# Products that nobody reads, in TensorE's waits between the end of attention and the sort of a one-core decoder layer

## What is computed

```python
x = x + linear_attention(layernorm(x))            # 16 heads, running sums of k v over the 64 rows
x = x + autocorrelation_attention(layernorm(x), ctx)   # see below
x = x + moe_ffn(layernorm(x))                     # 8 experts, top 2, sort by expert, gated up and down products
```

## Time and profile before

| | |
|---|---|
| median of three runs | 636.89 us (636.69 to 638.78) |
| the profiled execution's own time | 637.31 us |
| its span, first to last instruction | 635.5 us |
| TensorE busy | 570.0 us, 90% of the span |
| VectorE (DVE) busy | 517.7 us, 81% |
| GpSimd (POOL) busy | 427.1 us, 67% |
| ScalarE (ACT) busy | 420.1 us, 66% |
| mean granted TensorE clock | 0.947 of full speed |
| TensorE's share of the chain that ended last | 62% |

### The profile page before, as it was taken

One profiled execution on the slowest core, in us unless ns is written; L12 is line 12 of the kernel. 1 busy time (PEld: TensorE's weight loads), 2 busy tenths in 40 slices (PEclk: granted clock), 3 DMA queues, 4 the chain that ended last, 5 costly groups with the idle time before them and its releaser, 6 DMA issues.

```text
span 635.5 us, 15657 instructions
## 1 busy us (share of the span) xinstructions
PE 570.0 (90%) x3750; PEld 448.5 (71%) x3751; DVE 517.7 (81%) x1602; ACT 420.1 (66%) x1188; POOL 427.1 (67%) x461
## 2 busy tenths in 40 slices
PE   3899999999999999786899767799999999999993
PEld 1455555555555555455789754599999999989993
DVE  5699999999999999972678878566778887877883
ACT  4557877877787775441788512344788888878882
POOL 3899989998999899110877600765367666756762
PEclk9999999999999999955799859999999999999998
DMA  5510111111161111363477542222012111111110
GB/s 147 190 43 0 35 33 36 33 33 33 33 99 33 34 33 35 86 98 87 118 206 203 111 102 38 49 49 50 23 50 53 47 47 51 49 40 47 55 44 23
DMA packets 49972, 40.90 MB, mean 64 GB/s; under 512 B 21971, under 2 KB 40278, under 8 KB 49926
## 3 DMA queue, kind: packets, MB, share of 16 engines
q1 hardware_dynamic: 44150, 29.61, 18.8%
q0 software_dynamic: 4960, 10.49, 6.3%
q10 hardware_dynamic: 816, 0.26, 0.2%
HBM read 27.47 MB, written 12.88 MB: 63 GB/s over the span
## 4 chain that ended last, share of the span: by engine, by line
PE 62%; ACT 13%; DVE 12%; issue 6%; DMA 3%; POOL 2%; DVEq 0%; ACTq 0%; POOLq 0%; SPq 0%
PE bank L1329 55%; PE bank L1333 4%; ACT xh L671 3%; ACT xs L773 2%; DVE on L935 2%; PE bank L1545 2%; ACT nb_c L668 1%; ACT ex L647 1%; PE bank L1468 1%; DMA shared<-xs_d,row_u 1%; DVE R L896 1%; ACT rl L648 1%; ACT xrT L759 1%; ACT ex L653 1%; ACT v L650 1%
## 5 line engine op out<-in xcount | busy, mean ns | idle before, releaser
L542 POOL TENSOR_TENSOR shared<-v,qk 128x1152 f32<-128x1152 f32 x64 | 142.7, 2230 | 2.8
L1329 PE MATMUL bank<-shared,tri_s 128*128 128x360 f32 (+1 forms) x384 | 136.3, 491 | 0.8 <-DVE R L896 0.8
L609 POOL DMA_INDIRECT shared<-xs_d,row_u x91 | 87.9, 966 | 64.0 <-DVE row_u L1227 32.7
L896 DVE TENSOR_TENSOR R<-bank,qk 128x360 f32<-128x360 f32 (+1 forms) x192 | 96.1, 540 | 7.4 <-PE bank L1329 5.5
L1329 PEld LDWEIGHTS bank<-shared,tri_s 128*128 128x128 f32 x384 | 69.5, 192 | 44.9 <-issue 20.4
L616 POOL DMA_INDIRECT out_x<-shared x64 | 63.5, 993 | 48.3 <-DVE shared L1299 21.7
L905 DVE TENSOR_REDUCE nd<-R 128x144 f32<-128x1152 f32 x64 | 86.2, 1347 | 1.6
L1329 PE MATMUL bank<-w_s,hid 128*128 (+1 forms) x620 | 82.3, 276 | 0.0
L1329 PEld LDWEIGHTS bank<-w_s,hid 128*128 128x128 f32 x620 | 75.5, 192 | 0.6 <-issue 0.3
L812 ACT ACTIVATE shared<-bank 128x256 f32<-128x256 f32 x155 | 59.4, 384 | 21.7 <-PE bank L1329 16.2
L1320 DVE TENSOR_TENSOR hid<-bank,shared 128x256 f32<-128x256 f32 x155 | 61.6, 422 | 11.6 <-ACT shared L812 11.6
(11 more groups left out here) (245 smaller groups left out, 1146.0 us busy)
## 6 DMA issues: line engine op xcount, KB each, us to landing
xs_d<-xs SPq DMA_DIRECT2D x16, 270.0 KB, 5.0
X<-in_x SPq DMA_DIRECT2D x16, 256.0 KB, 2.8
ct<-in_ctx_t SPq DMA_DIRECT2D x16, 256.0 KB, 2.9
ct<-in_ctx_r SPq DMA_DIRECT2D x16, 256.0 KB, 3.6
gram_d<-gd SPq DMA_DIRECT2D x14, 256.0 KB, 2.4
w_s<-in_w_experts SPq DMA_DIRECT2D x8, 384.0 KB, 3.9
circ<-prob_d SPq DMA_DIRECT2D x30, 64.0 KB, 2.7
shared<-xs_d,row_u POOLq DMA_INDIRECT x91, 2.5
```

What stands on the lines that cost most here:

```text
L542: nc.gpsimd.tensor_tensor(outer[k], v9[k % 2][:].unsqueeze(3).broadcast_to([P, H, D1, D]), kk.unsqueeze(2).broadcast_to([P, H, D1, D]), AL ...
L609: nc.gpsimd.indirect_dma_start(xg[q], None, xs_d[:, :], bass.IndirectOffsetOnAxis(ap=rows, axis=0)).then_inc(xg_in[q], 16)
L896: nc.vector.tensor_tensor(R[:, lo:hi], bank[2 + c][:, 0:n_h * D1 * D].rearrange("p (h e d) -> p h e d", h=n_h, e=D1), qq.unsqueeze(2).broa ...
L1329: return nc.tensor.matmul(o, l, r, start=start, stop=stop, skip_group_check=True)
```

## The change

`keep_warm` moves ahead of the slots and takes a bank and a number. Its operands become `ones3` on both sides (bf16 ones, 128 x 128, the moving side read four times over, so 512 columns as before). It is called at twelve more places, which makes 88 more products in all: 10, 2, 6 and 2 in slots 16 and 17 of attention (bank 2, which the running sums have left; a wait on `b_mul` stands ahead of the first); 18 between the mean's early and late product, 6 ahead of the fifth value product and 8 behind it (bank 7); 3 behind each of the circulant products 0 to 3 (bank 7); 4 behind the last circulant product, 5 at the start of slots 16 and 17, 3 behind the counts of slot 16, 3 and 4 behind those of slot 18 (bank 0). The calls in the sort keep bank 5 and their numbers.

```diff
--- before.py
+++ after.py
@@ -1348,6 +1348,11 @@
                 need(pe, a_pev, 3 * t)
                 mm(bank[1][:, 0:3 * E], xT[:, k * P:(k + 1) * P], wqkv[:]).then_inc(a_proj, 1)
 
+            def keep_warm(of, times):
+
+                for _ in range(times):
+                    mm(bank[of][:], ones3[:], ones3[:].unsqueeze(1).broadcast_to([P, 512 // P, P]))
+
             def slot(n, i):
                 a1, b, c, d = (stage(n, i, s) for s in (1, 0, -1, -2))
                 if i is None and n == 0:
@@ -1379,9 +1384,14 @@
                     mm(bank[7][:], wkk[:, 0:E], ct[p][:]).then_inc(d_k, 1)
                 if a1:
                     project(*a1, 1)
+                if i is None and n == NG:
+                    pe.wait_ge(b_mul, 3 * NT)
+                    keep_warm(2, 10)
                 if c:
                     pe.wait_ge(c_on, c[0] + 1)
                     transposes(bank[5], on).then_inc(c_tr, 1)
+                if i is None and n == NG:
+                    keep_warm(2, 2)
                 if b:
                     running_sums(*b, 2)
                 if c:
@@ -1398,8 +1408,12 @@
                     project(*a1, 2)
                 if d:
                     g, p, r = d
+                    if i is None and g == NG - 1:
+                        keep_warm(2, 6)
                     pe.wait_ge(d_xh, GT * g + GT)
                     transposes(bank[5], xh2).then_inc(d_tr, 1)
+                    if i is None and g == NG - 1:
+                        keep_warm(2, 2)
                 if b:
                     running_sums(*b, 3)
                 if a1:
@@ -1442,14 +1456,20 @@
                 v_product(*grp(g))
             pe.wait_ge(mean_ch, 1)
             mm(bank[4][:, 0:L], ones_f[:], mean_early[:], True, False)
+            keep_warm(7, 18)
             pe.wait_ge(mean_ch, MEAN_READY)
             mm(bank[4][:, 0:L], ones_f[:], mean_late[:], False, True).then_inc(mean_mm, 1)
             mm(bank[3][:, 0:L], late_of, mean_late[:]).then_inc(mean_mm, 1)
             for g in range(EARLY_V, PRE):
+                if g == PRE - 1:
+                    keep_warm(7, 6)
                 v_product(*grp(g))
+            keep_warm(7, 8)
 
             def cross_slot(n):
                 v, e, f, sc = (cross_stage(n, k) for k in (1, 0, -2, -3))
+                if n in (NG, NG + 1):
+                    keep_warm(0, 5)
                 if e:
                     g, p, r = e
                     pe.wait_ge(e_u, g + 1)
@@ -1458,6 +1478,10 @@
                     for k in range(GT):
                         last = mm(bank[2][:, k * P:(k + 1) * P], circ[p][:, k, :], u_of(g)[:, k, :])
                     last.then_inc(e_y, 1)
+                    if g < PRE - 1:
+                        keep_warm(7, 3)
+                    if g == NG - 1:
+                        keep_warm(0, 4)
                 if v and v[0] >= PRE:
                     v_product(*v)
                 if f:
@@ -1485,20 +1509,19 @@
                         last = mm(counts[:, (k + 1) * NPAIR:(m + 1) * NPAIR], ones_b[:],
                                   picked[:, t + k:t + k + 1, 0:NPAIR].broadcast_to([P, m - k, NPAIR]), False, k == m - 1)
                     last.then_inc(s_cnt, 1)
+                    if t + m == NT:
+                        keep_warm(0, 4)
+                    elif n >= NG:
+                        keep_warm(0, 3)
 
             pe.wait_ge(setup, 11)
             cross_slots(cross_slot)
-
-            def keep_warm(times):
-
-                for _ in range(times):
-                    mm(bank[5][:], ones_b[:], picked[:, 0:512 // NPW, :])
 
             pe.wait_ge(r_ch, START_READY)
             mm(bank[0][:, 0:NPAIR], ones_f[0:NPAIR, :], wide_f[0:NPAIR, 0:NPAIR]).then_inc(r_mm, 1)
             pe.wait_ge(r_ch, TILE_READY)
             mm(bank[2][:, 0:NXI], ones_f[0:NPAIR, :], wide_f[0:NPAIR, NPAIR:2 * NPAIR]).then_inc(r_mm, 1)
-            keep_warm(16)
+            keep_warm(5, 16)
             for b in range(NT // NSORT):
                 pe.wait_ge(o_low, b + 1)
                 pe.wait_ge(o_part, b + 1)
@@ -1507,15 +1530,15 @@
                     last = mm(bank[1][:, 0:P], is_row[b % 2][:, k // 2, :, :, k % 2], is_low[b % 2][:, k // 2, :, k % 2],
                               b + k == 0, b * NSORT + k == NT - 1)
                 last.then_inc(o_mm, 1)
-                keep_warm(4 if b < NT // NSORT - 1 else 2)
+                keep_warm(5, 4 if b < NT // NSORT - 1 else 2)
             pe.wait_ge(r_ch, ROWS_READY)
             mm(bank[3][:, 0:NT + NXI], row_t, select[:]).then_inc(r_mm, 1)
             pe.wait_ge(r_ch, BEGUN_READY)
             mm(bank[4][:, 0:5 * NT], ones_f[0:NPAIR, :], begun[0:NPAIR].rearrange("p m j -> p (m j)")).then_inc(r_mm, 1)
-            keep_warm(4)
+            keep_warm(5, 4)
             pe.wait_ge(r_ch, MASK_READY)
             nc.tensor.transpose(bank[6][:, 0:P], new_mask[:], id_s[:]).then_inc(r_mm, 1)
-            keep_warm(6)
+            keep_warm(5, 6)
 
             packs_pe = [None, None]
 
```

## The result

| | before | after |
|---|---|---|
| runs, median | 638.23 us (6 runs, 636.69 to 638.78) | 633.38 us (6 runs, 632.29 to 634.77) |
| profiled execution | 637.31 us, span 635.5 | 633.54 us, span 631.7 |

The ratio is 0.9928 with an interval of 0.9912 to 0.9944: faster by 0.7%, against the 633.1 us forecast. The changed kernel was run again beside the experiments (e0): 633.08 us, ratio 0.9904 [0.9875, 0.9934].

What follows compares the result with a forecast made beforehand. PE at half clock was taken to bound nearly every PE step from 267 to 309 us, besides DMA, and the last groups from 360 to 372. Gains 0.81 + 0.31 + 1.11 + 2.0 = 4.23 off 637.31 gave 633.1, range 631.4 to 636.8.

Steps and rivals of the forecast that it cites:

- Transposes, products, last gram: End of attention: everything behind the output products 1.5 us earlier, 2.4 us with the last gram; its dummies cost nothing.
- The open wait: Between the value products and the early mean's product: PE has nothing for 2.9 us, without a dummy.
- The 18 dummies: Between early and late mean's product: they block the late one for 1.6 us, so it gains 0.81 instead of 2.4.
- Late product to DVE's next step: From the late mean's product to DVE's next step: 0.73 us becomes 0.42, a gain of 0.31.
- Store and load of the weights: DVE and two DMAs up to the first circulant product: 8.74 us unchanged, PE's work hidden with about 0.9 us margin.
- Circulant products: Circulant products 0 to 3: the first saves 0.91 us, the next transposes just 0.2, together 1.11.
- Last slots: Last transposes and scores ahead of DVE's last choice: DVE starts 2.05 us earlier, taken as 2.0.
- the fall in the open wait: Rival, 0.24: clock falls ahead of the early mean's product, 6 to 13 dummies run slow; 634.2 to 635.9 us.
- All given back: Rival, 0.07: early sum earlier or the 18 dummies shorter, nothing overruns; 5.9 us gained, so 631.4.
- Not held: Rival, 0.13: five dummies don't keep the clock up at the last slots, the 2.0 is lost; 635.1 to 636.8 us.
- Slower: Rival, 0.06: clock stays low in both places, dummies block at half rate, over 0.26 us each; up to 642.0 us.
- No effect: Rival, 0.05: the clock falls all the same and the dummies fit; 637 us.

Runs made afterwards that it cites:

- e0: The changed kernel run again without edit, as yardstick of the first group: 633.08 us, ratio 0.9904.
- e10: The changed kernel run a third time without edit, as companion of the third group: 632.38 us, ratio 0.9916.
- traces with ten: Profiled executions of four runs with 10 instead of 18 dummies between the mean's early and late product, two of them with further edits.
- e6: Changed kernel with the six dummies of the fifth value product moved ahead of the third, so the context load issues late: 634.45 us, ratio 0.9940.
- e1: Changed kernel with 10 instead of 18 dummies between the mean's early and late product: 631.62 us, ratio 0.9890.
- e2: Changed kernel with 26 instead of 18 dummies between the mean's early and late product: 636.65 us, ratio 0.9973.
- e8: Changed kernel with 10 instead of 18 dummies, and two instead of six at the end of the sort: 632.66 us, ratio 0.9927.
- e9: Same file as e1 run again, 10 instead of 18 dummies in the changed kernel: 632.14 us, ratio 0.9905.
- e4: Changed kernel without the dummies of the last slots, keeping those from attention's end to the fourth circulant product: 634.44 us, ratio 0.9942.

## Why the prediction was right, and where it was not

The time came as forecast, 633.4 for 633.1, by terms of which some were too large and some too small. Measured from where PE enters the stretch, the profiled execution gained 5.06 us, where the sum was 4.23. Term by term:

- **Transposes, products, last gram.** Right. The last gram ends 10.43 us behind the start of the transposes of `on` (278.72 + 0.69 - 268.98); before it was 12.81 (279.38 + 1.12 - 267.69), 2.4 more, as worked out. The ten dummies left 0.63 of their wait open, as worked out.
- **The open wait.** Foreseen as one of 2.9 us ahead of the early mean's product; it came as two, 2.25 ahead of the value products and 0.68 ahead of the early mean's. The forecast let the value products follow the gram at once, but they waited for context, whose load did not move forward with the gram: it was issued 9.37 us behind the transposes of `on`, 9.03 before.
- **The 18 dummies.** The new wait is there in the form foreseen: the chain comes through the early sum and the block. Its size was off, 0.95 us (0.78 in e10) for 1.6. Seen from the transposes of `on`, the block was over 0.25 us sooner than worked out (19.90 for 287.84 - 267.69 = 20.15), as the early diagonals took 9.4 us from their issue at 268.11 to the sum, not 9.7. And the late sum was over 0.4 later (287.93 - 268.98 = 18.95; the product that waits for it was worked out for 286.25 - 267.69 = 18.56). There the step that failed in this execution is "the store, load and late sum behind it move along": the diagonals' store and load were issued 3.41 us apart (280.08 and 283.49), 3.03 before. What slowed the store was not tested; in the five other traces with eighteen the two are 3.00 to 3.23 apart. The term became 1.06 for 0.81. It is not a steady one: in those five traces the early sum starts 8.06 to 8.87 us behind the transposes of `on` (8.56 here), and the term is 0.38 to 1.53. The traces with ten show that the overrun is on the path.
- **Late product to DVE's next step.** 0.36 for 0.31.
- **Store and load of the weights.** The forecast moved these 8.74 us without a change and asked only whether PE's work fits beside them. It did not ask which transfers run beside the store. That is the missed term: 1.03 us, the store's own 1.19 (2.71 to 1.52), shown by e6, less 0.16 by which the load of `circ` behind it took longer (2.93 to 3.09). PE's work beside them was hidden as foreseen, with 0.84 to spare. The prediction had followed the context load as PE's wait, not as the store's neighbour.
- **Circulant products.** 1.02 for 1.11. The third product waited 2.10 us for its own load (4.00 us in the chain), which the forecast did not have, and the three dummies behind it held the first group's transposes until 304.44. Neither set the step: in e10 the third product started 4.40 us behind the first, for 5.87 here, those transposes were not held, and the step was 10.41 for 10.40. There the chain runs through GpSimd's scale and shift of the second group, as the forecast had it.
- **Last slots.** 1.17 for 2.0. The price was right where the clock held (1.98 in e10); the step that failed is taking the full 2.0 after naming, two sentences earlier, that the clock may fall in slot 17. In the changed kernel's profiled execution the clock fell 0.6 us before the second scores. With the same five dummies the stretch from the last transposes to the last choice took 4.04 to 4.08 us in five traces (after, e1, e2, e8, e9) and 3.24 to 3.29 in three (e0, e6, e10), for 5.25 before: the 2.0 was had in three of eight.
- **The missed 1.03 and the 0.83 too much** of the last slots nearly cancel. The base helped too: the forecast went by the profiled execution's 637.31, while six runs of the kernel before have a median of 638.23, so that 4.23 off the median would have been 634.0. The gain was 4.85 for 4.23. The hit on the total is in part luck; the sign of each term of the sum was right.

The rivals: the fall in the open wait happened in e0 and cost 0.5 us, since most of its low stretch fell on work with time to spare; its price went wrong by taking the low stretch to begin with the block. "All given back" (631.4) is near what ten reaches (631.96): the overrun was real, and not needed. "Not held" is half true: in three profiled executions of the changed kernel the clock fell once ahead of the last scores, once between them and once behind them. "Slower" needed a pitch over 0.26 us in the block; it was 0.216. "No effect" is ruled out by the interval.

The low clock itself costs little here: 44.4 us fewer at half rate (61.45 - 17.06) brought 5.06. The Trainium skill (TensorE: Matmul & The Clock Gate, Terms) would price that at half, 22 us; in this kernel the measurement decides for a fourth of that, as most of those stretches wait for DMA, DVE and ACT.

## What to carry to other kernels

Before filling a wait with unread products, find what is queued behind them on the engine and when its data come; the count to choose ends a little before that, and too many cost their full price (26 against 18 moved the product that was read by 1.73 us, 8 x 0.216). Price a faster stretch by the product and transfer on the chain that it moves, and ask which transfers then run beside each other, not by the time at the low clock. Compare medians of many runs when the gain hangs on where a clock falls, since one profiled execution can be off by more than a microsecond.

## What was not expected of the hardware

- The edges of the clock lie elsewhere in each execution of one kernel. In the three profiled executions of the changed kernel the clock, held up to there but for the fall in e0, fell at 366.09, 359.88 and 375.15 around the last slots; at the start the same six products took 4.05, 3.07 and 3.79 us.
- A store of 64 KB landed in 1.52 to 1.55 us with a load of 256 KB issued 1.6 us ahead of it (nine traces), and in 2.58 to 2.75 with that load 0.4 us ahead (three); in e2 it took 2.70 us with the load 1.6 us ahead and one packet of instruction fetch beside it.
- PEclk read 1.00 at the start of both executions while products took about twice their later time: a clock that is low there is seen in durations only.
- Of eleven profiled executions with the front filled only two, e0's and e4's, lost the clock there, and both not in an open wait but about a microsecond after it (2.04 and 2.14 us long), with PE at work again. The changed kernel's own waits of 2.25 and 2.10 us passed without a fall.
